# The next head's q projection behind the four score blocks, and its ScalarE half behind the exponentials

## The reference, cut to what matters

```
q = einsum('bsh,he->bse', x, w_q)            # 16 heads of 128
k, v = split(einsum('bsh,he->bse', x, w_kv)) # 4 groups of 128
scores = einsum('bqgpd,bkgd->bgqpk', q, k) * SCALE
scores = where(causal, scores, -inf)
probs = softmax(scores)
ctx = einsum('bgqpk,bkgd->bqgpd', probs, v)
return einsum('bse,eh->bsh', ctx, w_dense)
```

## Time and profile before

| | |
|---|---|
| median of 3 runs | 2614.89 us (2613.47 to 2616.02) |
| the profiled execution's own time | 2615.02 us |
| its span in the trace | 2613.2 us |
| busy share of the span: PE, PEld, DVE, ACT, POOL | 96%, 88%, 83%, 36%, 35% |
| granted TensorE clock, mean | 0.988 |

### The profile page before, as it was taken

The page is one execution under the profiler, slowest core; times in us unless marked ns, Lnnn a source line. Parts: engine busy times, 40 slices in busy tenths (PEclk is TensorE's granted clock), DMA queues, the critical chain, the costliest instruction groups (busy, mean ns, idle before and its releaser), DMA issues. The chain is left out here.

```text
span 2613.2 us, 45221 instructions
## 1 busy us (share of the span) xinstructions
PE 2511.2 (96%) x14116; PEld 2298.0 (88%) x14116; DVE 2155.9 (83%) x6164; ACT 945.1 (36%) x2546; POOL 910.6 (35%) x1950
## 2 busy tenths in 40 slices
PE   6999999999996899999999999997999999999998
PEld 6999999999995788888888888886899999999997
DVE  6888888888886888888888888886888888888887
ACT  3111101101102777777777777774111101101100
POOL 4332332332323444343434344334332332332321
PEclk9999999999998999999999999997999999999999
DMA  6000000000001554454545554455100000000000
GB/s 191 11 1 1 1 1 1 1 1 1 1 25 49 91 92 91 86 94 90 87 92 91 92 92 91 85 98 127 34 9 1 9 9 1 9 9 1 9 9 9
DMA packets 378735, 117.25 MB, mean 45 GB/s; under 512 B 338560, under 2 KB 377472, under 8 KB 378496
## 3 DMA queue, kind: packets, MB, share of 16 engines
q1 hardware_dynamic: 378496, 114.36, 21.9%
HBM read 26.24 MB, written 4.19 MB: 12 GB/s over the span
## 5 line engine op out<-in xcount | busy, mean ns | idle before, releaser
L555 PE MATMUL ffn_ring<-ffn_mix_weights,ffn_yT 128*128 128x384 f32 x5760 | 1155.7, 341 | 6.7 <-DVE ffn_mix_weights L790 4.3
L555 PEld LDWEIGHTS ffn_ring<-ffn_mix_weights,ffn_yT 128*128 128x128 f32 x5760 | 1007.4, 189 | 57.5 <-DVE ffn_mix_sums L725 15.8
L727 DVE SCALAR_TENSOR_TENSOR ffn_mix_sums<-ffn_ring,ffn_w,ffn_mix_sums 128x384 f32<-128x384 f32 x896 | 550.3, 614 | 243.0 <-PE ffn_ring L555 226.1
L605 PE MATMUL ffn_ring<-ffn_out_weights,ffn_avT 128*128 128x512 f32 x1536 | 442.3, 399 | 6.2 <-POOL ffn_avT L1028 4.5
L1547 ACT ACTIVATE attn_exponentials<-attn_exponentials,attn_score_neg_max 128x512 f32<-128x512 f32 (+3 forms) x512 | 285.8, 559 | 173.5 <-DVE attn_score_neg_max L1462 172.9
L1614 POOL CAST attn_probsT_long<-attn_turned_long 128x1024 fp32r<-128x1024 f16 (+1 forms) x256 | 232.4, 936 | 248.0 <-DVE attn_probs L1479 246.8
L605 PEld LDWEIGHTS ffn_ring<-ffn_out_weights,ffn_avT 128*128 128x128 f32 x1536 | 282.8, 189 | 36.0 <-POOL ffn_avT L1028 5.7
L1479 DVE SCALAR_TENSOR_TENSOR attn_probs<-attn_exponentials,attn_prob_factor,attn_probs 128x512 f16<-128x512 f32 (+3 forms) x512 | 254.0, 557 | 20.2 <-ACT attn_probs L1556 19.9
L1556 ACT ACTIVATE attn_probs<-attn_exponentials,attn_prob_factor 128x512 f16<-128x512 f32 (+3 forms) x512 | 250.2, 552 | 23.1 <-DVE attn_prob_factor L1472 13.8
L742 DVE SCALAR_TENSOR_TENSOR x<-ffn_ring,ffn_w_out,x 128x256 f32<-128x256 f32 x512 | 246.9, 482 | 12.0 <-PE ffn_ring L605 5.3
L1302 PE MATMUL attn_scores<-attn_kT,attn_qT 128*128 128x512 f32 (+2 forms) x1152 | 243.2, 338 | 9.1 <-DVE attn_qT L1445 7.6
(11 more groups left out here) (149 smaller groups left out, 3263.1 us busy)
## 6 DMA issues: line engine op xcount, KB each, us to landing
ffn_mix_stage<-in_L_ffn_q_proj_dram SPq DMA_DIRECT2D x32, 128.0 KB, 2.5
ffn_mix_stage<-in_L_ffn_k_proj_dram SPq DMA_DIRECT2D x32, 128.0 KB, 2.6
ffn_mix_stage<-in_L_ffn_v_proj_dram SPq DMA_DIRECT2D x32, 128.0 KB, 2.9
ffn_out_stage<-in_L_ffn_o_proj_dram SPq DMA_DIRECT2D x16, 256.0 KB, 3.2
out_dram<-x SPq DMA_DIRECT2D x8, 512.0 KB, 2.9
x<-in_L_attn_x_dram SPq DMA_DIRECT2D x7, 512.0 KB, 8.2
early_stage<-in_L_attn_w_q_dram SPq DMA_DIRECT2D x4, 512.0 KB, 5.7
attn_dense_stage<-in_L_attn_w_dense_dram SPq DMA_DIRECT2D x4, 512.0 KB, 4.7
```

What stands on the lines that cost most here:

```text
L555: last = pe.matmul(bank[:, 0:QKV], yT[:, t % 2, h, k * P:(k + 1) * P], mix_half(e, wh)[:, k], start=(n == 0), stop=(n == 3 * CK - 1))
L605: last = pe.matmul(bank[:], avT[:, t % 2, h], wo[:, g, wh], start=(i == 0), stop=(i == 2))
L727: dve.scalar_tensor_tensor(into, bank[:, 0:QKV], w[:, t, e:e + 1], into, ALU.mult, ALU.add).then_inc(mix_done, 1)
```

## The change

On TensorE place B moves from between scores 2 and 1 to behind scores 0. On ScalarE exponentials 1 and 0 move ahead of places B and C. VectorE's order, the transfers and the work itself stay as they were. The removed lines shift the line numbers of ScalarE's part by one (1541, 1547, 1556 and 1562 become 1540, 1546, 1555 and 1561).

```diff
@@ block.tensor, slot @@
                 if now:
                     scores(now, 3)
                     scores(now, 2)
-                place("B")
-                if now:
                     scores(now, 1)
                     scores(now, 0)
+                place("B")
                 place("C")
@@ block.scalar, slot @@
                 if now:
                     exponential(now, 3)
                     exponential(now, 2)
+                    exponential(now, 1)
+                    exponential(now, 0)
                 place("B")
-                if now:
-                    exponential(now, 1)
                 place("C")
-                if now:
-                    exponential(now, 0)
                 place("D")
```

## The result

The changed kernel took 2683.6 us (median of 5 runs, 2681.2 to 2684.99), the kernel before 2613.47 us on the same chip (5 runs). The ratio is 1.0268, 95% interval 1.0255 to 1.0281. The forecast was 2685.5 us. The profiled execution took 2681.2 us, its span is 2679.4 us: 66.2 us longer than before.

What follows compares the result with a forecast made beforehand. The prediction took a loop through VectorE and ScalarE, closed by the q low half, to bound plain slots. Items 1 to 6 +53.8, item 7 +8.6 and item 0 +8.3 gave +70.7 us, forecast 2685.5, range 2660 to 2702.

Steps and rivals of the forecast that it cites:

- The loop: VectorE and ScalarE: max 3, exponentials 3 and 2, q halves, reciprocal and factor, split_probs, max 3; period Q + 3.61.
- plain slot: Slot with nothing but the q projection in it, such as item 4 head 13; period forecast at 7.53 us.
- Q: Distance of VectorE's q low half from the start S of its widest score_max; forecast 3.92 in heads 0 to 14.
- ScalarE's part: Exponentials 1 and 0 ahead start ScalarE's q half at S+3.30 in place of S+2.42; +0.88 us in a plain slot.
- TensorE's part: Earlier scores 1 and 0 on TensorE end VectorE's 22.8 us of waits, already contained in the smaller losses of late slots.
- The rival that had the kernel faster: VectorE's 22.8 us of waits for scores disappear and nothing takes their place: 2592 us; chance 0.04.
- The slots where TensorE set the pace: Heads 5 to 8, next S late by TensorE; after the change 7.53, 7.53, 7.62, 7.93 us, TensorE falling behind nowhere.
- The sum: Whole kernel: +53.8 us for items 1 to 6, +8.6 for item 7, +8.3 for item 0, together +70.7.
- likeliest case: The forecast itself, with no error but in the start-to-start distances: 2676 to 2695 us; chance 0.82.
- The clock: Rival: TensorE's idle time lets its clock fall in one slot of each item, +40 us, 2726; chance 0.04.
- The 1.7 us of idle time: TensorE was forecast to stand idle for some 1.7 us of a plain slot after the change, busy 5.9 of 7.5.
- The highest occupancy: Skill's rule alone points at TensorE, 98%: the kernel would stay at 2615 or win what TensorE's neighbours stop waiting for.

Runs made afterwards that it cites:

- half dose: Changed kernel with exponential 0 put back behind places B and C on ScalarE, exponential 1 still ahead of the q half; 2642.86 us, ratio 1.0112 to the kernel before.
- the kernel with the reciprocal ahead: Changed kernel with prob_rsum 2 moved ahead of the q low half on VectorE; 2642.13 us, ratio 1.0106 to the kernel before.
- the changed kernel with the smaller dense product: Changed kernel with the third term of TensorE's dense product left out, 4 matmuls of 12 per slot; 2684.47 us, ratio 1.0273 to the kernel before.

## Why the prediction was right

**The loop.** The prediction said that a plain slot's pace is the chain from max 3 over the q half and the reciprocal back to max 3, with a period of Q + 3.61, and that Q would become 3.92 and the period 7.53. Measured: 3.91 and 7.52. The half dose (3.52 and 7.14) and the kernel with the reciprocal ahead (Q = 3.91, but 6.63 for the plain slot and 7.05 for a v slot, both 7.52 with the change) show the two members of the claim apart: the half sets the time, and it does so through what is queued behind it on VectorE.

**ScalarE's part.** "+0.88 in every plain slot": measured +0.87 to +0.89 in most slots of heads 9, 10, 12 and 13, less in most of the others (the slot of before had waited for late turned probabilities, or was one of item 7) and 1.13 in one, item 0 head 12. That the loss is ScalarE's is shown by ScalarE's part alone, 2686.8.

**TensorE's part.** I said that VectorE's 22.8 us of waits for scores go, but are contained in the smaller losses of those slots and can't be subtracted again. With TensorE's part alone they went and the time stayed: other waits took their place. The rival that had the kernel faster is out.

**The slots where TensorE set the pace.** Predicted for heads 5 to 8: 7.53, 7.53, 7.62, 7.93. Measured in item 4: 7.52, 7.52, 7.52, 7.88. TensorE fell behind nowhere; with 58 us of its work removed the changed kernel did not gain.

**The sum.** Predicted +53.8 for items 1 to 6, +8.6 for item 7 and +8.3 for item 0, 70.7 in all. Measured +52.2 (757.5 us for six items against 705.2), +8.2 and +8.5, 68.9. The one visible miss is k slots: heads 3, 7 and 11 were forecast at 8.21, 7.62 and 8.60 and took 8.10, 7.52 and 8.48. Before, the k low half waited for ScalarE's k half; behind the late q half that half is ready, and VectorE starts 0.1 earlier. (The 0.1 is read from the starts, item 4 head 3: the k low half came 0.97 us behind the q low half and now comes 0.87 behind it.) I had noted that these waits shrink and not put it in the sum: 2 us.

That the forecast of 2685.5 came within 1.9 us of the median is in part luck. Single executions of the changed kernel differ by 3.8 us, and the medians of before, 2614.89 in the prediction and 2613.47 beside the changed kernel, by 1.4. The width of the likeliest case was not worked out either: 0.05 us in 120 slots is 6 us, not the 9.5 at either side of 2685.5. The measured time lies inside both.

**The clock.** The window of the changed kernel's steady part:

```profile
868.00:1842.00 974.00, 902.12 (x5303) 780.39 (x5302) 774.13 (x2562) 701.44 (x1843) 362.26 (x554) 1.00 0.47 85
```

The granted clock, third from the end, is 1.00 as before, the 2.4 GHz level, although TensorE waits 0.75 us before the dense product of the plain slot above and 1.3 and 1.6 us in the slots of heads 2 and 14. The case of the clock did not come about. Two things qualify it. In item 0, where TensorE waits 7.1 us for a q low half, the clock is lower than before: 0.54 and 0.65 in the slots of heads 1 and 2, against 0.69 and 0.79. And the case was nearer than the prediction's argument makes it: with less work for TensorE, waits of 2.1 us were followed by the 1.2 GHz level in six slots of the changed kernel, which became up to 0.7 us longer. The 1.7 us of idle time that the prediction gave TensorE in a plain slot were not seen: in item 4 head 13 its rows fill 6.77 of 7.52 us, and 0.75 is the whole of its pause.

**The highest occupancy.** TensorE's 98% was no sign of the bound for most slots. Taking some 58 us off TensorE gave 20 before the change and nothing after it. The Trainium skill (Perfetto Trace Analysis, Identifying the Most-Contended Engine) says to optimize the engine of highest occupancy first and to judge TensorE by its weight loads; read from matmul time, this case's 98%, the rule would have pointed at TensorE for a change that costs 70 us on ScalarE's side. In the changed kernel no engine stands out: in the middle stretch VectorE is busy for 79%, ScalarE for 72%, and TensorE for 92% by its matmuls and 79% by its weight loads.

## What to carry to other kernels

When two engines hand work back and forth, look for the small instruction that is queued behind an item from the other engine: its wait is passed on even if it needs nothing of that item. Here a reciprocal of 0.15 us stood behind a projection half, and moving two exponentials ahead of that half cost 0.88 us in a loop of 6.65. To price such a reordering, write one slot as start-to-start distances, close the loop, and ask only when its late member starts now; then check apart the slots in which another engine sets the pace, since a wait removed there can come back one slot later, or before another item.

## What the runs showed of the hardware that was not expected

Matmul busy time differed for the same matmuls: 921.56 us in the changed kernel's 5385 matmuls between the first and last widest score_max, 902.02 us in the 5385 before, at a granted clock of 0.99 both times. It was the longer, the longer the stretch with its pauses was: 903.3 us with TensorE's part alone (a stretch of 938.2 us), 913.1 with the half dose (966.3), 923.2 with ScalarE's part alone (1011.0). The weight loads' time shows no such order: 799 us before, 793, 795 and 805 in these three, and 797 in the changed kernel. In these kernels they are the steadier measure of TensorE's work; why the matmul rows lengthen is not shown.

TensorE's clock fell to the 1.2 GHz level behind six of 14 waits of 2.1 us in the changed kernel with the smaller dense product, and behind none of the 14 waits of 1.2 to 1.7 us at the same places in the changed kernel. Taking work off an engine that already waits can so give nothing back.

ScalarE's activations kept fixed distances. Start to start, exponentials of 384, 256 and 128 columns took 0.61, 0.49 and 0.39 us in the slots looked at, equal to their durations, and that is why a sum of three such distances came out to 0.01 us. The read of the sum has a part in it: it starts some 0.1 us before the exponential ends, and the next instruction 0.09 behind the start of the read (1451.48 and 1451.57 above). The q half, which gathers no sum, lets the next instruction start 0.48 us behind it for a duration of 0.58.
